# Attention, feed-forward and two layer norms on eight cores: weight loads moved from ACT's queue to SP's, and a fourth softmax buffer

## What is computed

```python
q = rope((x @ Wq.T).reshape(B, S, 32, 128).transpose(0, 2, 1, 3))
K, V = k_cache[block_table], v_cache[block_table]   # 8 heads, 4096 keys, each for 4 query heads
scores = einsum('bhsd,bhkd->bhsk', q, K) / sqrt(128)
ctx = einsum('bhsk,bhkd->bhsd', softmax(scores, -1), V)
x = layernorm(x + ctx @ Wo.T)
w = broadcast_to(kernel[None, :], (8, COMPRESSED)).reshape(4096, 4096)   # values -1, 0, 1
x = layernorm(x + x @ w)                            # x is (4, 4096, 4096)
```

## Time and profile before

| | us |
|---|---|
| Median of 3 runs | 10983.19 |
| Their range | 10929.97 to 11022.01 |
| The profiled execution | 10927.98 |
| Its span on core 5, the slowest | 10926.4 |
| Spans of all cores | 10764.7 to 10926.4 |
| P1 of group 1, first block to the start of P2 | 3765 to 4212 |
| P2 of group 1 | 4212 to 5323 |
| P3 of group 1 | 5331 to 5557 |
| PE, DVE, ACT, POOL busy | 5957.7, 3894.5, 2336.5, 2817.8 |
| Mean granted TensorE clock, core by core | 0.845 to 0.857 |

### The profile page before, as it was taken

One profiled execution on the slowest core, in us unless ns is written; L12 is line 12 of the kernel. 1 busy time (PEld: TensorE's weight loads), 2 busy tenths in 40 slices (PEclk: granted clock), 3 DMA queues, 4 the chain that ended last, 5 costly groups with the idle time before them and its releaser, 6 DMA issues.

```text
span 10926.4 us, 70316 instructions; the slowest of 8 cores (10764.7 to 10926.4 us)
## 1 busy us (share of the span) xinstructions
PE 5957.7 (55%) x25472; PEld 2524.4 (23%) x25472; DVE 3894.5 (36%) x2224; ACT 2336.5 (21%) x2216; POOL 2817.8 (26%) x1064
## 2 busy tenths in 40 slices
PE   0000046666607266666736666675566666937788
PEld 0000012111106122111532211134121112713333
DVE  0000011666600214666421366652126666121122
ACT  0000001555400003555200255530015554000000
POOL 0000000666500003666300266640016665000000
PEclk9999988888858688888968888887788888767788
DMA  9998741000085421000242100013310000331211
GB/s 109 137 137 146 162 106 66 16 16 16 10 186 166 133 77 39 16 16 8 81 141 89 46 16 16 16 48 142 106 62 16 16 16 16 116 123 62 77 64 67
DMA packets 820116, 791.04 MB, mean 72 GB/s; under 512 B 706625, under 2 KB 772162, under 8 KB 777282
## 3 DMA queue, kind: packets, MB, share of 16 engines
q1 hardware_dynamic: 785922, 396.46, 13.5%
q0 software_dynamic: 6208, 121.64, 8.8%
q10 hardware_dynamic: 27648, 268.45, 6.7%
HBM read 583.05 MB, written 260.05 MB: 77 GB/s over the span
## 4 chain that ended last, share of the span: by engine, by line
PE 36%; POOL 24%; DMA 14%; DVE 8%; another core or an unknown queue 7%; SPq 7%; issue 2%; ACT 1%; POOLq 0%; ACTq 0%; DVEq 0%
PE PA L178 36%; POOL acc L171 24%; SPq L164 7%; DMA slab<-wqT_s 6%; DVE recip L171 4%; DVE z L171 2%; DMA wqT_s<-slab 2%; DMA woT_s<-slab 2%; DMA x1b_s<-z 1%; ACT ebuf L171 1%; DMA z<-x_in 1%; DVE attnb L171 1%; DVE xcar L171 1%; DMA slab<-vc_in,idx 1%
## 5 line engine op out<-in xcount | busy, mean ns | idle before, releaser
L171 POOL TENSOR_TENSOR acc<-acc,ebuf 128x1024 f32<-128x1024 f32 x960 | 2729.7, 2843 | 367.3 <-ACT ebuf L171 245.4
L171 ACT ACTIVATE ebuf<-PA,konst 128x1024 bf16<-128x1024 f32 x2048 | 2241.8, 1114 | 2103.0 <-PE PA L178 1477.6
L171 DVE TENSOR_TENSOR acc<-acc,ebuf 128x1024 f32<-128x1024 f32 x960 | 2464.0, 2567 | 581.1 <-ACT ebuf L171 581.1
L178 PE MATMUL PA<-xcar,slab 128*128 128x512 bf16 x4096 | 1101.9, 436 | 2467.2 <-DMA xcar<-x_s 1979.3
L178 PE MATMUL PA<-ebuf,kvw 128*128 128x512 bf16 x4096 | 1295.5, 399 | 918.9 <-ACT ebuf L171 810.8
L178 PE MATMUL PA<-qTar,kvw 128*128 128x512 bf16 x4096 | 1330.1, 412 | 10.1 <-DVE qTar L171 10.1
L171 DVE TENSOR_TENSOR z<-PA,sing 128x512 f32<-128x512 f32 x128 | 88.5, 691 | 3113.9 <-PE PA L178 3113.9
L178 PE MATMUL PA<-kvw,xcar 128*128 128x512 bf16 x4096 | 993.3, 411 | 373.9 <-DMA xcar<-x1b_s 373.9
L178 PE MATMUL PA<-slab,xcar 128*128 128x256 bf16 x8192 | 945.9, 282 | 402.2 <-DMA slab<-woT_s 402.2
L178 PEld LDWEIGHTS PA<-xcar,slab 128*128 128x128 bf16 x4096 | 438.0, 109 | 3107.2 <-issue 2769.0
L171 POOL CAST acc<-ebuf 128x1024 f32<-128x1024 bf16 x64 | 66.6, 1040 | 3989.4 <-ACT ebuf L171 3970.1
(11 more groups left out here) (31 smaller groups left out, 1044.0 us busy)
## 6 DMA issues: line engine op xcount, KB each, us to landing
slab<-wqT_s ACTq DMA_DIRECT2D x128, 1024.0 KB, 4.8
slab<-woT_s ACTq DMA_DIRECT2D x64, 2048.0 KB, 7.8
wq_s<-wq_in POOLq DMA_DIRECT2D x4, 8192.0 KB, 233.7
wo_s<-wo_in POOLq DMA_DIRECT2D x4, 8192.0 KB, 226.9
wqT_s<-slab SPq DMA_DIRECT2D x32, 1024.0 KB, 8.0
kvw<-vg_s SPq DMA_DIRECT2D x32, 1024.0 KB, 5.4
woT_s<-slab SPq DMA_DIRECT2D x32, 1024.0 KB, 5.9
z<-x_in SPq DMA_DIRECT2D x16, 2048.0 KB, 7.6
```

Of the source, the lines that this page charges most:

```text
L171: getattr(e, m)(*a, **kw2).then_inc(c.h, 1))
L178: e.matmul(o, l, r, start=st, stop=sp).then_inc(c.h, 1))
```

## The change

Three edits. The loads of `wqTs` in P1 and of `woTs` in P3 are issued from SP instead of ACT, at the same place of the program. Their wait for a built weight is now SP's own wait for the stores of the build, so `fence_builds` and its semaphore go away. The order of the two waits ahead of each load is not the same everywhere, but both stand. And `ebuf` has four slots instead of three, used as `j % 4`.

```diff
-    ebuf = sbt("ebuf", [128, 3 * 1024], BF16)
+    ebuf = sbt("ebuf", [128, 4 * 1024], BF16)
@@
-    def fence_builds():
-        W("sync", sQ, sQ.v)
-        sFN.v += 1
-        _SCHED_META["sync"].append(("i", "sFN", 1))
-        E("sync", lambda e, v=sFN: e.nop().then_inc(v.h, 1))
@@
     wT_built = build_wT(wq16, wqTs, 128, wq_cast_all)
-    fence_builds()
-
-    ebuf_free_pe = [0, 0, 0]
-    ebuf_free_acc = [(None, 0), (None, 0), (None, 0)]
+
+    ebuf_free_pe = [0, 0, 0, 0]
+    ebuf_free_acc = [(None, 0)] * 4
@@ phase_p1
-            W("scalar", sFN, 1)
-            W("scalar", sGSt, gath_all)
-            W("scalar", sPE, slab_free[par])
+            W("sync", sQ, wT_built)
+            W("sync", sPE, slab_free[par])
             js = slab[:, par * 4096:(par + 1) * 4096]
-            c_js = DMA("scalar", sJS[par], js.rearrange("p (dc j) -> p dc j", j=128),
+            c_js = DMA("sync", sJS[par], js.rearrange("p (dc j) -> p dc j", j=128),
                        wqTs[jblk, :, :, :])
@@ phase_p2
-                    eslot = j % 3
+                    eslot = j % 4
@@ phase_p3
-            W("scalar", sPE, slab_free[par])
-            W("scalar", sFN, 2)
+            W("sync", sPE, slab_free[par])
+            W("sync", sQ, wT_built)
             cs = slab[:, par * 8192:(par + 1) * 8192]
-            c_cs = DMA("scalar", sCOL[par], cs.rearrange("p (c o) -> p c o", o=256),
+            c_cs = DMA("sync", sCOL[par], cs.rearrange("p (c o) -> p c o", o=256),
                        woTs[oblk, :, :, :])
```

More of the change, by code:

```diff
@@ L131, in build_nc @@
              "sCOL0", "sCOL1", "sZX", "sGX", "sGX0", "sGG", "sGW", "sGZ", "sGF",
-             "sVR", "sWB0", "sWB1", "sWB2", "sWB3", "sFN",
+             "sVR", "sWB0", "sWB1", "sWB2", "sWB3",
              "sPE", "sDVE", "sACT", "sPL")
@@ L143, in build_nc @@
     sVR = C["sVR"]
-    sFN = C["sFN"]
     dma_ctrs = [sQ, sK, sGSt, sXT, sCS, sJS[0], sJS[1], sKV[0], sKV[1],
```

## The result

The changed kernel takes 10261.79 us (median of 10 runs, 10092.76 to 10438.25), the kernel before 10985.31 (10 runs, 10858.14 to 11081.81). The ratio is 0.9252, with a 95% interval of 0.9109 to 0.9395. It is taken from executions in which no die of the chip was held at a lower TensorE clock than the other (two of the changed kernel's), since such executions differ by hundreds of us whatever the kernel; the medians above hold them all. The interval, 10006 to 10321 us, reaches into that range, and the median of all executions, 724 us lower than before, lies in it.

The account below looks back on a forecast made before the run. Bound: TensorE (36% of the chain) and GpSimd's adds (24%), with PE waiting 487.9 us for P1 weight loads. Forecast: 10928 - 710 + 48 + 55 = 10321 us, said as 10320; range 10180 to 10500.

Parts of the forecast that it names:

- The loads of P1: Query projection: weight loads issued from SP are hidden, blocks 8.3 us apart instead of 13.8; -698 us in four stages.
- The place behind the transposes: Start of P1: the first load now stands behind the transposes on SP, 3 us later per stage; +12 us, at most 35.
- The loads of P3: Start of P3: the first load lies under attention when issued from SP; 8.1 us in each of three groups, -24 us.
- The fourth buffer: Attention: an earlier exp doesn't shorten the alternating DVE and GpSimd adds; 0 us, bounds +260 and -40.
- The base: Whole kernel: the profiled execution's 10928 us as starting point, with 55 us added for its distance to the median of 10983.
- The price of the low clock: P1: a stage at clock 0.81 takes 48 us longer; one such stage of four expected on the slowest core, +48 us.
- the sum: Whole kernel at full clock: P1 loads -698, later first load +12, P3 loads -24, fourth buffer 0; -710 us.
- P1 at 0.81 in all stages: Rival for P1: all four stages run at the low clock, +192 us instead of +48; 10465 us, chance 0.18.
- Cold blocks: Rival for P1: the 1.04 us hole lowers the clock in each block, period 9.7 us; 10447 us, chance 0.07.
- late loads: Rival for P1: loads on SP's queue land late, at 11.3 us, period 9.25 us; 10391 us, chance 0.07.
- the slower outcome: Rival for P1: loads landing from 21 us on make the kernel slower; 11178 us at 24 us landing, chance 0.03.
- Adds at 3.34: Rival for attention: with four buffers the adds fall out of step, a pair costs 3.34 us; 10533 us, chance 0.04.

Follow-up runs that it names:

- the second profiles: The changed kernel and the unchanged kernel before, each run and profiled once more; at full clock 10072.81 us (fastest of six) against 10805.25 to 10814.49.
- the first experiment: Only the P1 weight loads moved from ACT to SP, against the kernel before; executions of 10201 to 10640 us beside 10851 to 11181.

## Why the prediction was right in its mechanism and too high in its number

**The loads of P1: right.** Forecast were -698 us in four stages. In the second profiles at full clock the stages of core 0, from first to last matmul, are 437, 438, 440 and 440 us before and 268, 267, 266 and 266 after, together -688. The period is 8.32 us against 8.3, the block 7.07 against 7.05, and the hole of 1.04 didn't let the clock fall.

**The place behind the transposes: no cost seen.** On the two cores profiled as slowest, and leaving out the first stage, PE waited (1979.3 - 1435.8)/3 = 181.2 us at the start of a P1 stage for `xcar`, and now (1998.3 - 1448.5)/3 = 183.3 for the slab. That looks like the 3 us that were taken, but it is not an effect of the change: over all cores of both profiles PE's pause between P3 and P1 is 183.4 us in the mean before (179.9 to 185.9) and 182.7 after (181.2 to 187.7). The +12 isn't there. K and V came in time; the pause between the last P1 matmul and the first of P2 is 4 us in both kernels.

**The loads of P3: right.** The step is 33.3 us before and 26.1 after, in the mean of all cores of both profiles: 7 us in three groups, against 8.1.

**The fourth buffer: right.** 0 to 2 us a stage, against nothing. ACT's wait for GpSimd fell from 623.3 to 382.5 us and moved nothing. That the two engines hold each other up was only argued from the earlier trace rows; it is shown by the adds on DVE alone, 1.22 us each. Whether they strictly take turns isn't: a pair costs less than both adds one after the other. The Trainium skill (SBUF — State Buffer, SBUF: two separate sides) says of a DVE operation with two SBUF inputs beside a GpSimd operation that reads SBUF: "the other fully blocks". The trace comes near to that: 3.07 us for what takes 2.12 + 1.22 = 3.34 one at a time.

**The base, the step that failed.** The prediction started from the 10928 us of the profiled execution, added 48 for a P1 stage at 0.81, and 55 for the distance to the median. It had read core 5's last P3 stage at 0.81 and used it as a price for P1, but not taken it out of the base. That stage and the feed-forward phase held 138 us that no part of the kernel requires. At full clock the base is 10928 - 138 = 10790, and 10790 - 710 = 10080; measured at full clock were 10072.81 and 10092.76. Against such executions the two additions put 103 us on top of the 138 already counted, 241 in all, which is the distance from 10321 to 10080. Over all runs, with the low clock in them as it comes, the median is 10262, 58 below the forecast. Nearly all of that is the 48 added: without it the forecast would have been 10983 - 710 = 10273.

The price of the low clock was right: a P1 stage at 0.81 throughout took 47 to 49 us more in the first experiment. (The 298 us of core 4's last P1 stage in the profile after are at 0.87, so only in part at the low clock.) Wrong was to treat it as an addition to a time that already had its share, and to look for it in P1 alone: in the profile after, core 4 lost 31 us in P1, 64 in two P3 stages and 108 in the feed-forward phase, 203 of its 10288.

The 822 us of the result can be taken apart as far as the record goes. 739 are the difference at full clock. The two executions of the changed kernel behind the ratio took 10092.76 and 10137.45 us, in the mean 42 above the 10073 at full clock; with 0.9252 those of before come to about 10933, which is 121 above the 10812 at full clock. That gives another 79, and applying the ratio to 10985 the last 4. So the executions of before that were compared held more of the low clock than those of the changed kernel; in which stages isn't on record.

That 10080 came so close is in part luck: the difference at full clock was 739 where the sum had 710, and the base was 10812 where 10790 had been worked out. The sum itself stands: on core 0 of the second profiles P1 gave 688 and the steps from P2 to P3 22, together 710. But those two spans differ by 678, mostly since the changed kernel's first P1 stage began 24 us later there (1438 against 1414) and its wait for the building of `woT_s` was 15 longer. Over the cores of the four profiles the first P1 stage begins at 1403 to 1466 us before and at 1403 to 1458 after, so a difference of two spans can't confirm the sum to better than tens of us.

**The rivals.** P1 at 0.81 in all stages is what the profile of the first experiment comes near to on its cores 0 and 5, so it can happen, but the second profile of the changed kernel has P1 stages of 266 to 271 us at 0.99 or 1.00 on all eight cores. The Trainium skill's rule on the peak-current limiter (TensorE: Matmul & The Clock Gate, Part 1), by which the whole die falls to 13/16 once three of its cores run dense matmuls, is thus met in some executions and not in others. Nor did the fall take whole dies: in the first profile of before, the last P3 stage took 267 and 268 us at 0.82 on cores 4 and 5, and 226 at 0.99 on cores 6 and 7 of the same die. Cold blocks, late loads and the slower outcome didn't happen: no P1 block but the first of a stage waited for a load, with landing at 4.8 us as before. Adds at 3.34 didn't happen either.

## What to carry to other kernels

Look at where a transfer stands in its engine's program before asking for more buffers: a double buffer is worth nothing while the load that fills it waits behind the consumer of the other half. A load can be moved ahead on its own queue or to another engine's; look then at what it will run beside, as the wait of 24.93 us beside K's fetch shows. A wait of 4 us in each block cost 5.5, since the matmuls behind it ran slowly, and a hole of 1 us cost only itself. And before a sum is made against a profiled execution, take out what that execution lost to the clock, stage by stage: a stage with the same matmuls twice in one trace, once at 0.99 and once at 0.82, or the same stage on another core, shows how much.

## What the runs showed of the hardware

- Adds of 128x1024 with two SBUF inputs: DVE alone 1.22 us, GpSimd without a DVE add beside it 2.12; side by side a pair every 3.07, and the recorded lengths (2.92 on GpSimd, 2.77 to 2.96 on DVE) hold the waiting too. Splitting the adds between the two engines was slower than giving all of them to DVE, 1083 against 910 us a stage.
- With a PE hole of 3.68 us before each block, the block of 32 matmuls took 9.59 us instead of 7.07; with one of 1.04 us it took 7.07.
- The granted clock of PE with all cores in dense phases was not one number: the same feed-forward phase took 1078 to 1084 us at 0.91 on some cores and 1179 to 1202 at 0.81 to 0.83 on others, within each of the two profiled executions of before. It came and went for pairs of cores (0 and 1, 2 and 3, 4 and 5, 6 and 7), in each of which both had it in the same stages. What decides it was not found. The stages before the change, with PE less dense, could be held low too, as the earlier trace rows showed: the first P1 stage of core 6 took 467 us, where core 4 took 439.
- A weight load of 1 MB, issued from ACT while SP's queue held a transposing fetch of K of 20.01 us, let PE start only 26 us after its issue; the median from issue to landing is 4.9 us in that kernel.
